# Downward product of two gated layers in three split passes, two rounds behind the upward products

## The reference, cut to what matters

```
HID = int(DIM * 4 * 2 / 3)            # 341
h = (h - mu) / jnp.sqrt(var + 1e-05) * lg + lb
h = h @ w1 + b1                       # 128 -> 682
a, g = jnp.split(h, 2, axis=-1)
h = a * jax.nn.gelu(g, approximate=False)
x = x + h @ w2 + b2                   # 341 -> 128
```

## Time and profile before

| | us |
|---|---|
| median of 3 runs | 1802.2 |
| the profiled execution | 1800.36 |
| its span, first to last instruction | 1798.6 |
| TensorE busy | 1685.2 (94%) |
| VectorE busy | 1379.1 (77%) |
| ScalarE busy | 1307.2 (73%) |
| GpSimd busy | 1124.5 (63%) |

### The profile page before, as it was taken

One profiled execution on the slowest core, in us unless ns is written; L12 is line 12 of the kernel. 1 busy time (PEld: TensorE's weight loads), 2 busy tenths in 40 slices (PEclk: granted clock), 3 DMA queues, 4 the chain that ended last, 5 costly groups with the idle time before them and its releaser, 6 DMA issues. The chain is left out here.

```text
span 1798.6 us, 43507 instructions
## 1 busy us (share of the span) xinstructions
PE 1685.2 (94%) x15560; PEld 1095.7 (61%) x15560; DVE 1379.1 (77%) x2368; ACT 1307.2 (73%) x4474; POOL 1124.5 (63%) x1011
## 2 busy tenths in 40 slices
PE   7998899999989999999899999799999999999999
PEld 4664577775557777655344444477776556777655
DVE  4553999994779999556788887799995688999745
ACT  4444688887448888755899998688887537888863
POOL 3653899994479999612322220799996278999730
PEclk7999999999999999999899999999999999999999
DMA  2001111102101110201755551311102102110111
GB/s 65 2 2 44 38 26 31 26 19 65 39 20 41 31 25 20 54 15 24 132 92 101 101 95 25 78 26 31 26 19 55 50 1 54 26 31 20 43 30 41
DMA packets 68573, 74.80 MB, mean 42 GB/s; under 512 B 14260, under 2 KB 52360, under 8 KB 66312
## 3 DMA queue, kind: packets, MB, share of 16 engines
q1 hardware_dynamic: 68360, 72.03, 18.9%
HBM read 27.99 MB, written 10.49 MB: 21 GB/s over the span
## 5 line engine op out<-in xcount | busy, mean ns | idle before, releaser
L436 POOL TENSOR_TENSOR rsum<-pa,pb 128x512 f32<-128x512 f32 x256 | 325.4, 1291 | 55.1 <-DVE pa L354 41.2
L818 ACT ACTIVATE ffn_prob<-sc,ffn_nmax 128x128 f32<-128x128 f32 x928 | 326.7, 387 | 5.3 <-DVE ffn_nmax L735 5.3
L902 POOL TENSOR_TENSOR ffn_prob<-ffn_prob,ffn_rden 128x512 f32<-128x512 f32 x256 | 265.2, 1057 | 71.6 <-DVE ffn_rden L750 71.4
L445 POOL TENSOR_TENSOR rsum<-rsum,ffn_rnt 128x512 f32<-128x512 f32 x256 | 261.5, 1042 | 10.9 <-ACT ffn_rnt L840 8.6
L818 ACT ACTIVATION_READ_ACCUMULATOR ffn_prob<-sc,ffn_nmax 128x1 f32 x928 | 210.3, 227 | 0.0
L364 DVE TENSOR_TENSOR pb<-proj,ffn_tab 128x512 f32<-128x512 f32 x236 | 161.0, 682 | 59.0 <-ACT rn L406 58.4
L344 PE MATMUL pt<-ident,rsum 128*128 128x128 f32 x960 | 154.1, 284 | 15.1 <-POOL rsum L445 12.3
L344 PEld LDWEIGHTS pt<-ident,rsum 128*128 128x128 f32 x960 | 100.7, 141 | 96.6 <-ACT ffn_ptb L826 70.5
L735 DVE TENSOR_REDUCE ffn_nmax<-sc 128x4 f32<-128x512 f32 x232 | 148.4, 680 | 13.6 <-PE sc L632 10.4
L373 DVE TENSOR_REDUCE ffn_ss<-rn 128x16 f32<-128x1024 f32 x128 | 154.2, 1205 | 0.0
L642 PE MATMUL pt<-ident,ffn_prob 128*128 128x128 f32 x1024 | 143.5, 277 | 11.3 <-POOL ffn_prob L902 11.0
(11 more groups left out here) (284 smaller groups left out, 4356.2 us busy)
## 6 DMA issues: line engine op xcount, KB each, us to landing
ffn_v<-ffn_v SPq DMA_DIRECT2D x128, 128.0 KB, 2.3
column_ks<-qk_parts SPq DMA_DIRECT2D x64, 128.0 KB, 4.1
rn<-Y SPq DMA_DIRECT2D x32, 128.0 KB, 2.3
qk_parts<-column_hi SPq DMA_DIRECT2D x64, 64.0 KB, 1.9
qk_parts<-column_lo SPq DMA_DIRECT2D x64, 64.0 KB, 1.9
column_qs<-qk_parts SPq DMA_DIRECT2D x32, 128.0 KB
column_qs<-qk_parts SPq DMA_DIRECT2D x64, 64.0 KB
rn<-Y SPq DMA_DIRECT2D x32, 127.5 KB, 2.4
```

What stands on the lines that cost most here:

```text
L436: pool.tensor_tensor(K.sm[:, r, w], K.m1[:, r, w], K.m2[:, r, w], ALU.add).then_inc(S.f_sum, 1)
L445: pool.tensor_tensor(heads(K.sm[:, r, w]), heads(K.sm[:, r, w]), K.rnt[:, r, w * HEADS:(w + 1) * HEADS].unsqueeze(2).broadcast_to([P, HEAD ...
L818: ins = act.activation(K.prob[:, r, e, k], score_banks(i)[e][:, tokens(k)], ACT.Exp, bias=K.nmax[:, r, e, k:k + 1], accum_out=K.den[:, r, ...
L902: pool.tensor_tensor(K.prob[:, r, e], K.prob[:, r, e], K.rden[:, r, e].unsqueeze(2).broadcast_to([P, 4, P]), ALU.mult).then_inc(S.f_pn, 1)
```

## The change

In the second and fourth layer the downward product is made of three passes, like the upward ones: high part of the weights by high part of `u`, high by low, low by high.

- GpSimd makes `K.w2_hi` and `K.w2_lo` once a layer (`split_down_weights`, four instructions), after its attention work and ahead of the eight additions.
- ScalarE makes the high part of `u` (`high_part`, L1127 of the changed kernel: a cast into `K.hhi`) after the `gelu` of the next round.
- GpSimd makes the low part (L992: `K.u` less its high part, into `K.hlo`), 24 times a layer.
- `down(x)` waits for the low part, and comes after `up(x+2)` (`lag` = 2) rather than after `up(x+1)`. So `down(22)` and `down(23)` stand behind the last `up`.
- `gate(x)` waits until the low part of round x-2 is made, and `high_part(x)` until `down(x-2)` is done.
- VectorE's `residual` moves from the first to the second round of a pair, and `gate_split` from the second to the first.

The first and third layer are as before. No DMA is added or taken away.

```diff
--- before.py
+++ after.py
@@ -290,6 +290,19 @@
     pool.wait_ge(S.wm_hi, 2 * n + 1)
     pool.tensor_tensor(K.w1_lo, K.stage1[:], K.w1_hi.bitcast(F32), ALU.subtract).then_inc(S.wm_hi, 1)
 
+
+
+def split_down_weights(pool, K, n):
+
+    S, at = K.s, 2 * (n // DEPTH)
+    pool.wait_ge(S.wm_in, MLP_LOADS * (n + 1))
+    pool.wait_ge(S.f_v, TILES * (n + 1))
+    rest = slice(0, HID - 2 * P)
+    pool.tensor_copy(K.w2_hi[:, 0:2], K.w2[:, 0:2])
+    pool.tensor_copy(K.w2_hi[rest, 2], K.w2[rest, 2]).then_inc(S.wd_hi, 1)
+    pool.wait_ge(S.wd_hi, at // 2 + 1)
+    pool.tensor_tensor(K.w2_lo[:, 0:2], K.w2[:, 0:2], K.w2_hi[:, 0:2].bitcast(F32), ALU.subtract).then_inc(S.wd_lo, 1)
+    pool.tensor_tensor(K.w2_lo[rest, 2], K.w2[rest, 2], K.w2_hi[rest, 2].bitcast(F32), ALU.subtract).then_inc(S.wd_lo, 1)
 
 
 TILES = 4 * PAIRS
@@ -932,6 +945,8 @@
                 pool.wait_ge(S.f_pn, 2 * TILES * n + 2 * i)
                 pool.memset(first_rows[:, PAIRS:2 * PAIRS], 0.0).then_inc(S.g_z, 1)
                 pool.wait_ge(S.g_z, 2 * n + 2)
+        if n % DEPTH:
+            split_down_weights(pool, K, n)
 
     return sync, tensor, vector, scalar, gpsimd
 
@@ -945,6 +960,8 @@
     final = n == 2 * DEPTH - 1
     feeds = last and not final
     summed = n // DEPTH * PAIRS
+    lag = 2 if last else 1
+    split = n // DEPTH * UPS
     up_bank = lambda x, side: K.pt[1 - side] if x == 2 else (K.proj if side else K.sc)[x if x < 2 else (x - 3) % 2]
 
     def sync(sp):
@@ -969,6 +986,10 @@
             for p in range(PAIRS):
                 pool.wait_ge(S.f_y, PAIRS * n + p + 1)
                 pool.tensor_tensor(K.X[:, pair(p)], K.X[:, pair(p)], K.Y[:, pair(p)], ALU.add).then_inc(S.f_xy, 1)
+            for x in range(UPS):
+                hn = HID_CHUNKS[x % NM][1]
+                pool.wait_ge(S.u_hi, split + x + 1)
+                pool.tensor_tensor(K.hlo[0:hn, x % 2], K.u[0:hn, x % 2], K.hhi[0:hn, x % 2].bitcast(F32), ALU.subtract).then_inc(S.u_lo, 1)
         if (n + 1) % DEPTH:
             split_query_key_weights(pool, K, n + 1)
             low_parts(pool, K, n + 1, 0)
@@ -1008,12 +1029,23 @@
         def down(x):
             p, m = divmod(x, NM)
             hn = HID_CHUNKS[m][1]
-            pe.wait_ge(S.u, UPS * n + x + 1)
+            if last:
+                pe.wait_ge(S.u_lo, split + x + 1)
+            else:
+                pe.wait_ge(S.u, UPS * n + x + 1)
             if m == 0:
                 if p >= 1:
                     pe.wait_ge(S.ff_y, PAIRS * n + p)
                 else:
                     pe.wait_ge(S.g_ln, PAIRS * n + PAIRS)
+            if last:
+                if x == 0:
+                    pe.wait_ge(S.wd_lo, 2 * (n // DEPTH + 1))
+                hi, lo = K.hhi[0:hn, x % 2], K.hlo[0:hn, x % 2]
+                pe.matmul(K.ob[:], K.w2_hi[0:hn, m], hi, start=(m == 0), stop=False)
+                pe.matmul(K.ob[:], K.w2_hi[0:hn, m], lo, start=False, stop=False)
+                pe.matmul(K.ob[:], K.w2_lo[0:hn, m], hi, start=False, stop=(m == NM - 1)).then_inc(S.dn, 1)
+                return
             pe.matmul(K.ob[:], K.w2[0:hn, m], K.u[0:hn, x % 2], start=(m == 0), stop=(m == NM - 1)).then_inc(S.dn, 1)
 
         def early(x):
@@ -1054,8 +1086,8 @@
         for x in range(UPS):
             if x >= 3:
                 up(x)
-            if x >= 1:
-                down(x - 1)
+            if x >= lag:
+                down(x - lag)
             if (n + 1) % DEPTH:
                 early(x)
             if feeds and x == 6:
@@ -1065,7 +1097,8 @@
                 column_variance(pe, K, 0)
             if final and x >= 5 and x % 3 == 2:
                 turn_output((x - 5) // 3)
-        down(UPS - 1)
+        for x in range(UPS - lag, UPS):
+            down(x)
         if final:
             turn_output(PAIRS - 1)
         if (n + 1) % DEPTH:
@@ -1086,9 +1119,18 @@
             act.wait_ge(S.fin_t, p + 1)
             act.copy(K.tok[:, 4 * p:4 * p + 4, :], K.pt[p % 2][:].rearrange("p (q c) -> p q c", c=P)).then_inc(S.fin_out, 1)
 
+        def high_part(x):
+            hn = HID_CHUNKS[x % NM][1]
+            act.wait_ge(S.u, UPS * n + x + 1)
+            if x >= 2:
+                act.wait_ge(S.dn, UPS * n + x - 1)
+            act.copy(K.hhi[0:hn, x % 2], K.u[0:hn, x % 2]).then_inc(S.u_hi, 1)
+
         for x in range(UPS + 1):
             if x < UPS:
                 gelu(x)
+            if last and x >= 1:
+                high_part(x - 1)
             if feeds and x == 7:
                 column_square(act, K, 0)
             if final and x >= 6 and x % 3 == 0:
@@ -1114,7 +1156,10 @@
             dve.wait_ge(S.up, 2 * UPS * n + 2 * x + 2)
             dve.wait_ge(S.gl, UPS * n + x + 1)
             if x >= 2:
-                dve.wait_ge(S.dn, UPS * n + x - 1)
+                if last:
+                    dve.wait_ge(S.u_lo, split + x - 1)
+                else:
+                    dve.wait_ge(S.dn, UPS * n + x - 1)
             dve.scalar_tensor_tensor(K.u[0:hn, x % 2], up_bank(x, 0)[0:hn, :], K.colb[0:hn, 2 * m:2 * m + 1],
                                      K.gl[0:hn, x % 2], ALU.add, ALU.mult).then_inc(S.u, 1)
 
@@ -1146,9 +1191,9 @@
         for x in range(UPS):
             p, m = divmod(x, NM)
             gate(x)
-            if m == 0 and p >= 1:
+            if m == lag - 1 and p >= 1:
                 residual(p - 1)
-            if m == 1 and 1 <= p and p + 1 < PAIRS:
+            if m == 2 - lag and 1 <= p and p + 1 < PAIRS:
                 gate_split(dve, K, n, p + 1)
             if (n + 1) % DEPTH:
                 early(x)
@@ -1962,6 +2007,10 @@
         self.up = new("up")
         self.gl = new("gl")
         self.u = new("u")
+        self.wd_hi = new("wd_hi")
+        self.wd_lo = new("wd_lo")
+        self.u_hi = new("u_hi")
+        self.u_lo = new("u_lo")
         self.dn = new("dn")
         self.ff_y = new("ff_y")
         self.a_zero = new("a_zero")
@@ -2061,6 +2110,7 @@
         K.sq, K.hs = K.rn[:, 0], K.rn[:, 1]
         K.qT = sb("qT", [P, 2, CHUNKS, PAIR])
         K.kT = sb("kT", [P, 2, CHUNKS, PAIR])
+        K.w2_hi, K.w2_lo = (x[:, 2, 0:3 * P].rearrange("p (m c) -> p m c", c=P) for x in (K.wqkv_hi, K.wqkv_lo))
         K.normed, K.shifted = (x[:].rearrange("p b c t -> p (b c t)") for x in (K.qT, K.kT))
 
         K.stage = K.v[:].rearrange("p a b c -> p (a b c)")
```

## The result

| | before | changed |
|---|---|---|
| median of the runs beside each other, us (15 runs each) | 1806.01 (1801.31 to 1812.41) | 1813.76 (1808.55 to 1817.17) |
| ratio of the two, 95% interval | | 1.0042 [1.0032, 1.0052] |
| profiled execution, us / its span | 1800.36 / 1798.6 | 1812.55 / 1810.8 |
| second layer, start of the first `up` to start of the last residual | 58.3 | 61.5 |
| fourth layer, the same | 58.1 | 62.1 |

The change makes the kernel 0.42% slower; the two medians lie 7.75 us apart. In the profiles the two stages account for 3.2 + 4.0 = 7.2 of that and the tail for 0.5. The first and third layers' rounds take 73.2 to 73.3 as before. The time forecast was 1808, and the changed kernel's median lies 5.8 above it and outside the range of 1802 to 1812.

A forecast was written before the change was run, and what follows sets the result against it. TensorE was taken to set the pace. Losses of 2.55 us (second layer) and 3.2 (fourth), together 5.7, took 1800.36 to 1806.1; with the median 1.8 above the profiled execution, forecast 1808, 8-in-10 range 1802 to 1812.

The forecast's parts named there:

- What it can give, 0.15 a round: Second and fourth layers' rounds: three passes take 0.70 instead of 0.85 us; at most 7.1 us in both layers.
- The way of `u`: Within a round: gelu, gate, cast (0.618), low part (1.27) reach TensorE at 3.53 us, wanted at 3.50; no slack.
- The meeting of GpSimd and VectorE: Steady rounds: VectorE's split and GpSimd's low part exclude each other; three rounds 6.79 instead of 6.75, 0.2 us lost a layer.
- The handing over in both directions: GpSimd and VectorE exclude each other but overlap 0.2 us at the change-over; one direction from the trace, the other estimated.
- The beginning: First rounds of second and fourth layer: `down(0)` waits for the low part, `up(3)` 1.03 late; 0.9 us lost a layer.
- The ends: Last rounds, nothing beside the longer way of `u`: 2.1 us more in the fourth layer, 1.45 in the second.
- The weights' parts: GpSimd's four instructions before the eight additions, about 2.3 us: cost nothing; up to 0.8 if they reached into `gate_split`.
- The starting point: Base of the forecast time: profiled execution 1800.36 us, with the median of the runs 1.8 above it.
- second rival: Steady rounds: exclusion holds to an instruction's very end; 6.99 a group, 1.2 us more a layer, 1810.3 in all; chance 0.17.
- lock to the very end: The second rival's mechanism in steady rounds: VectorE and GpSimd exclude each other for whole instructions, 6.99 a group; chance 0.17.
- Hardly meet: First rival, steady rounds: VectorE and GpSimd hardly collide; 1.6 us gained a layer, 1804 in all; chance 0.23.
- within 0.5%: Whole kernel: change smaller than the 9 us a measurement can tell from none; chance 0.87, slower 0.11, faster 0.02.

## Why the prediction was wrong, point by point

- **What it can give, 0.15 a round.** Right: the passes are 0.23 apart, and where nothing waits three rounds are 6.25.
- **The way of `u`.** Right: cast 0.607 for 0.618, low part 1.289 for 1.27, `down(0)` 2.0 us later after the first `up` than before, forecast 2.05 to 2.16.
- **The meeting of GpSimd and VectorE.** Right in mechanism and size: `ghi` at 1.41, where 0.9 to 1.4 was given, three rounds at 6.76 where 6.79 was forecast, so 0.1 or less of the 0.2 us a layer lost. In the fourth layer the same sum holds with the turning on top. The handing over in both directions, an estimate there, is seen: 0.48 us of `ghi` end at 1770.37, so it ran from 1769.89, 0.19 before GpSimd's end at 1770.08; the low part of 1770.85 ran from about 1772.32 - 1.29 = 1771.03, 0.12 before `glo`'s end.
- **The beginning. This is the step of the mechanism that failed.** It was priced at 0.9 a layer and cost 1.7 and 2.0 (the stages' growth less that of the end, the steady rounds being even). The late start itself was right: with the idle time filled, the second pass of `up(3)` is 1.01 late (forecast 1.03) and that of `up(4)` 0.85 and 0.86 (forecast 0.9). But the forecast let TensorE go on at 0.233 a pass after standing still for 2.1 us, and the granted clock fell to 0.55 and 0.64 over the 4 to 5 us behind it, with passes 0.43 apart. The Trainium skill (TensorE: Matmul & The Clock Gate, "Part 1: The HAM clock gate") gives two levels and, for 512 columns at the lower one, 426.7 ns from start to start. The trace agrees with 0.43. Filling the idle time gives back 1.2 and 1.1 of the stages.
- **The ends.** Right: +1.98 in the fourth layer (forecast 2.1), +1.5 in the second (1.45).
- **The weights' parts.** Nothing, as forecast: 1.8 us of GpSimd ahead of the additions (1724.8 to 1726.6), which end at 1736.5, 7 us before the first `up`.
- **The tail.** Not in the sum: the last turning 0.46 longer, at the lower clock, in both profiles of the changed kernel, but not in that of the kernel with the same fourth layer.
- **The starting point. This is the larger part of the miss.** The forecast added 5.7 to the median of three runs, 1802.2. Beside the changed kernel, and in each later group, the same kernel's median was 1804.4 to 1806.0. Of the 5.8 us by which 1808 fell short, 3.8 are this, and 7.75 - 5.7 = 2.0 is the change: 2.3 for the clock, 0.5 for the tail, less some 0.8 of terms priced too high. From 1806.0 the same sum would have given 1811.7, inside the range of 1802 to 1812.

The sum of both stages grew by 7.2, which is within the 3 to 8 that the forecast had named as its limits, though at their upper end and above its 5.7. The measured time lies beyond the second rival's 1810.3, but not by its mechanism: "lock to the very end" is refuted by 6.76 a group instead of 6.99. "Hardly meet" is refuted by `ghi` at 1.41. The chances put 0.87 on "within 0.5%", and the ratio of 1.0042 [1.0032, 1.0052] lies at the edge of that.

## What to carry to other kernels

When an added hand-over makes TensorE wait for about 2 us once, as here, price the wait and then look whether the few microseconds behind it run at the lower clock; here that cost more than the late start itself. A product that needs no preparation, put into that gap, saved both. A pipeline that gains in its steady rounds pays at its two ends: leave the old form in the rounds where nothing covers the longer way. And when two waits stand side by side, one edit alone can show half of the gain or none; try both together before giving either up. Last, a base of three runs was 0.2% off here, half of what the change was worth.
